# An audio-tower layer on Trainium2: score units of 28 to a sequence made 24, with a head's third and first query tile in one PSUM bank

## The reference

```python
# 1 token mixing: a causal convolution of 32 decaying taps gives 376 tokens, then two linear maps
h = _L0_tok_ref(x, Wv, bv, Wo, bo, decay_w)
# 2 attention, 16 heads of 16 features, causal, on the normalised h
q, k, v = (split(_layernorm(h) @ w + b) for w, b in ((wq, bq), (wk, bk), (wv, bv)))
scores = einsum('bhqd,bhkd->bhqk', q, k) / sqrt(16)
weights = softmax(where(tril(ones((s, s))), scores, -inf))
h = h + einsum('bhqk,bhkd->bhqd', weights, v).reshape(b, s, d) @ wo + bo
# 3 a feed-forward part: 2 shared experts and 16 routed ones, top 2 of a token
h = h + _L0_ffn_ref(_layernorm(h), ...)
```

## Time and profile before

| | |
|---|---|
| median of three runs | 1868.26 us (1855.72 to 1869.14) |
| span of the profiled execution | 1852.8 us |
| PE busy | 1700.5 us, 92% of the span |
| DVE busy | 1437.1 us, 78% |
| POOL busy | 1056.0 us, 57% |
| ACT busy | 976.7 us, 53% |

### The profile page before, as it was taken

How to read it: one execution, slowest core, us unless ns; L and a number is a source line. 1 busy time by engine, 2 the same in 40 slices (tenths; PEclk the granted TensorE clock), 3 DMA queues, 4 the chain that set the end, 5 groups by cost and what they waited for, 6 DMA issues and landing times. The chain is left out here.

```text
span 1852.8 us, 49530 instructions
## 1 busy us (share of the span) xinstructions
PE 1700.5 (92%) x14718; PEld 1360.0 (73%) x14719; DVE 1437.1 (78%) x3985; ACT 976.7 (53%) x2048; POOL 1056.0 (57%) x1446
## 2 busy tenths in 40 slices
PE   5899999999999999999999998589999986988883
PEld 4677777777777777777777775368888876877773
DVE  4589899999999899899999996378888971455554
ACT  1166666666676666666666765333444422544441
POOL 4045555555555655655555556446777770567666
PEclk8899999999999999999999999679999997999996
DMA  2555556556556555555565453223333356999996
GB/s 76 80 132 152 141 128 158 142 119 166 141 135 144 147 147 138 135 154 142 123 162 141 123 147 99 109 74 105 126 120 120 122 155 169 286 327 326 323 331 220
DMA packets 226548, 291.13 MB, mean 157 GB/s; under 512 B 57142, under 2 KB 188954, under 8 KB 226458
## 3 DMA queue, kind: packets, MB, share of 16 engines
q1 hardware_dynamic: 190042, 186.14, 40.3%
q0 software_dynamic: 18048, 49.31, 8.2%
q10 hardware_dynamic: 18368, 54.64, 7.7%
HBM read 83.25 MB, written 129.69 MB: 115 GB/s over the span
## 5 line engine op out<-in xcount | busy, mean ns | idle before, releaser
L752 ACT ACTIVATE probs<-bank 128x376 f32<-128x376 f32 (+2 forms) x896 | 440.7, 529 | 272.9 <-PE bank L621 261.0
L843 DVE TENSOR_REDUCE neg_max<-bank 120x1 f32<-120x376 f32 (+2 forms) x896 | 507.0, 587 | 53.7 <-PE bank L587 49.7
L587 PE MATMUL bank<-k_rows,q_rows 64*128 64x128 f32 (+2 forms) x1536 | 403.7, 345 | 3.1 <-ACT probs L752 2.4
L621 PE MATMUL bank<-q_rows,k_rows 64*120 64x120 f32 (+2 forms) x1536 | 369.9, 336 | 3.9 <-ACT probs L752 3.6
L982 POOL TENSOR_SCALAR_AFFINE_SELECT probs<-probs 128x512 f32<-128x512 f32 (+1 forms) x384 | 232.4, 631 | 209.5 <-ACT probs L752 209.3
L604 PE MATMUL bank<-causal,own_row 56*120 56x56 bf16 (+4 forms) x1792 | 300.9, 248 | 8.7 <-DMA k_rows<-k_flat_hi 3.5
L587 PEld LDWEIGHTS bank<-k_rows,q_rows 64*128 64x128 f32 (+1 forms) x1536 | 246.2, 186 | 6.7 <-ACT probs L752 4.6
L2205 POOL DMA_INDIRECT y_got<-y_sorted,p_route x188 | 182.4, 970 | 119.7 <-issue 117.6
L621 PEld LDWEIGHTS bank<-q_rows,k_rows 64*128 64x128 f32 (+1 forms) x1536 | 229.8, 183 | 8.7 <-ACT probs L752 5.8
L604 PEld LDWEIGHTS bank<-causal,own_row 64*128 64x128 bf16 (+2 forms) x1792 | 153.4, 115 | 110.3 <-DVE neg_max L843 39.9
L1847 POOL DMA_INDIRECT x_sorted<-r_normed,route x188 | 184.3, 981 | 83.6 <-issue 59.0
(11 more groups left out here) (235 smaller groups left out, 4148.8 us busy)
## 6 DMA issues: line engine op xcount, KB each, us to landing
x_sorted<-zeros ACTq DMA_DIRECT2D x32, 816.0 KB, 3.8
y_sorted<-zeros ACTq DMA_DIRECT2D x32, 816.0 KB, 4.3
x_rows<-x_sorted SPq DMA_DIRECT2D x51, 512.0 KB, 6.4
y_sorted<-p_y_rows SPq DMA_DIRECT2D x51, 512.0 KB, 6.4
q_rows<-q_flat_hi SPq DMA_DIRECT2D x256, 94.0 KB
k_rows<-k_flat_hi SPq DMA_DIRECT2D x248, 94.0 KB
q_rows<-q_flat_lo SPq DMA_DIRECT2D x128, 94.0 KB
out_dram<-base SPq DMA_DIRECT2D x47, 256.0 KB, 5.0
```

Of the source, the lines that this page charges most:

```text
L587: last = eng.matmul(ps[0:T[t], m * w:(m + 1) * w], q[rows, slot, t * P:t * P + T[t]], k[rows, slot, 0:w], start=False, stop=(m == len(head ...
L621: last = eng.matmul(ps[0:T[t], m * w:(m + 1) * w], k[64 * c:64 * c + 64, slot, t * P:t * P + T[t]], q[64 * c:64 * c + 64, slot, t * P:S], ...
L752: eng.activation(probs[g % 2][0:T[t], first:first + len(heads), OFF[t]:OFF[t] + w], bank_exp[n % 2][0:T[t], 0:len(heads) * w].rearrange("k ...
L843: eng.tensor_reduce(dst, src, AX.X, ALU.max, negate=True).then_inc(max_taken, 1)
```

## The change

A group has 6 units in place of 7. The first two hold two heads' middle tiles each. Each of the other four holds the third and the first query tile of one head: for the maxima 376 columns (384 with the mask's) and 128, for the exponential 376 and 120 columns, next to each other in the bank and in `probs`, so that one ACTIVATE of 496 columns does both. The reduce over such a bank gives four partial maxima, and a small reduce at the head of `turn_maxima` joins three of them. The rows of k and the last query tile are padded to 128, so that no matmul of scores has a shorter tile. Dense blocks stand at other units: conv0 and conv1 are now together at unit 7, ahead of the transposes; hid0 and hid1 are together; q0 and q1 are together at 13; k0 and k1 at 15. The order of POOL's masks is 1, 0, 2, the first two pieces of a reciprocal move, and `load_x` moves ahead in SP's queue.

```diff
-    GROUPS, UNITS = 4, 7
+    GROUPS, UNITS = 4, 6
-    OFF = [0, CUT[0], CUT[0] + CUT[1]]
+    OFF = [0, CUT[0] + CUT[2], CUT[0]]
-        k_rows = [sb(f"k_rows{p}", [P, 8, S], F32R) for p in range(2)]
+        k_rows = [sb(f"k_rows{p}", [P, 8, SPAN], F32R) for p in range(2)]
-        neg_max = sb("neg_max", [P, NT, 2, 8])
+        neg_max = sb("neg_max", [P, 2, 8, 6])
-                return (["hid0", "hid1"] * front + ["val0"] * maxima
+                return (["hid0", "hid1"] * front + ["val0"] * maxima + ["conv0", "conv1"] * mix
                         + ["nT0", "nT1", "q0", "q1", "k0", "k1"] * front
-                        + ["out0", "out1"] * finish + ["conv0", "conv1"] * mix + ["val1"] * maxima)
+                        + ["out0", "out1"] * finish + ["val1"] * maxima)
-        MAX_UNITS = [(0, (0, 1, 2, 3)), (1, (0, 1)), (1, (2, 3)), (2, (0,)), (2, (1,)), (2, (2,)), (2, (3,))]
...
+        PAIRS = 2
+        VALUES_AT = (3, 11, 16, 21)
...
                 def scores_for_max(st, g, u, m):
+                    if u < PAIRS:
+                        slot, t, at = 4 * (g // 2) + 2 * u + m, 1, 2 * P * m
+                    else:
+                        slot, t, at = 4 * (g // 2) + u - PAIRS, (2, 0)[m], NT * P * m
+                    keys = min(S, (t + 1) * P)
+                    last = eng.matmul(ps[:, at:at + keys], q[rows, slot, t * P:(t + 1) * P], k[rows, slot, 0:keys],
+                                      start=False, stop=(m == 1), skip_group_check=True)
...
                 def exps(st, g, u):
+                    if u < PAIRS:
+                        dst = probs[g % 2][:, 2 * u:2 * u + 2, OFF[1]:OFF[1] + CUT[1]]
+                        src = bank_exp[n % 2][:, 0:2 * CUT[1]].rearrange("k (m w) -> k m w", m=2)
+                    else:
+                        dst = probs[g % 2][:, u - PAIRS, 0:CUT[0] + CUT[2]]
+                        src = bank_exp[n % 2][:, 0:CUT[0] + CUT[2]]
+                    eng.activation(dst, src, ACT.Exp).then_inc(exp_done, 1)
...
                 def maxima(st, g, u):
+                    if u < PAIRS:
+                        src = max_bank(n)[:, 0:4 * P].rearrange("q (m w) -> q m w", m=2)
+                        dst = neg_max[:, half, 4 * e + 2 * u:4 * e + 2 * u + 2, 4]
+                    else:
+                        src = max_bank(n)[:, 0:4 * P].rearrange("q (c w) -> q c w", c=4)
+                        dst = neg_max[:, half, 4 * e + u - PAIRS, 0:4]
...
                 def turn_maxima(st, half, shift):
+                    eng.tensor_reduce(neg_max[:, half, :, 5], neg_max[:, half, :, 0:3], AX.X, ALU.min).then_inc(max_joined, 1)
+                    eng.wait_ge(max_joined, done)
...
                 # PE, step
-                        if n == 7 and st.maxima:
+                        if n == 5 and st.maxima:
                             values(st, 0)
+                        if n == 7 and st.mix:
+                            conv(st, 0)
+                            conv(st, 1)
                         if n == 9 and st.front:
                             normed_T(st, 0)
                             normed_T(st, 1)
-                        if n in (13, 15) and st.front:
-                            query_key(st, "q", (13, 15).index(n), w_q)
-                        if n == 17 and st.front:
+                        if n == 13 and st.front:
+                            query_key(st, "q", 0, w_q)
+                            query_key(st, "q", 1, w_q)
+                        if n == 15 and st.front:
                             query_key(st, "k", 0, w_k)
                             query_key(st, "k", 1, w_k)
-                        if n in (20, 22) and st.finish:
-                            out_rows_(st, (20, 22).index(n))
-                        if n in (24, 27) and st.mix:
-                            conv(st, (24, 27).index(n))
-                        if n == 27 and st.maxima:
+                        if n in (18, 20) and st.finish:
+                            out_rows_(st, (18, 20).index(n))
+                        if n == 23 and st.maxima:
                             values(st, 1)
...
                 # DVE
-                HALF_1_AT = {10: (0, 1), 12: (2,), 14: (3,), 16: (4,)}
-                HALF_0_AT = {21: (0,), 23: (1, 2), 25: (3,), 26: (4,)}
+                HALF_1_AT = {9: (0,), 11: (1,), 12: (2, 3), 13: (4,)}
+                HALF_0_AT = {19: (0,), 21: (1,), 22: (2, 3), 23: (4,)}
...
                 # POOL
-                            for t in reversed(range(NT)):
+                            for t in (1, 0, 2):
                                 mask(st, g, t)
```

More of the change, by code:

```diff
@@ L468, in attention_phase @@
         assert LOOP_FROM + 2 * LOOPS + 2 < B
-        MAX_UNITS = [(0, (0, 1, 2, 3)), (1, (0, 1)), (1, (2, 3)), (2, (0,)), (2, (1,)), (2, (2,)), (2, (3,))]
[L476 to L480, removed]
+        PAIRS = 2
+        VALUES_AT = (3, 11, 16, 21)
         def max_bank(n):
-            return bank_max[1 if n == LAST_UNIT else n % 3]
-        def units_since_same_bank(n):
-            return {0: 4, 1: 2, 2: 4, LAST_UNIT: 2}.get(n, 3)
+            return bank_max[n % 3]
         with nc.Block() as block:
@@ L595, in hide_later_keys @@
                     ps = max_bank(g * UNITS + u)
-                    t, heads = MAX_UNITS[u]
-                    w, d, m = KEYS_OF[t], T[t], len(heads)
                     rows = slice(64 * (g % 2), 64 * (g % 2) + 64)
+                    if u < PAIRS:
+                        blocks = ps[:, 0:4 * P].rearrange("q (m w) -> q m w", m=2)[:, :, P:2 * P]
+                    else:
+                        blocks = ps[:, 2 * P:4 * P].rearrange("q (m w) -> q m w", m=2)
                     for h in (1, 0):
[L601 to L604, removed]
+                        eng.matmul(blocks[:, :, 64 * h:P], own_row[rows, h, :], causal[rows, h, 0:2, 64 * h:P],
                                    start=(h == 1), stop=False, skip_group_check=True)
@@ L635, in scores @@
                         open_exp(st, g, u)
-                    for m in range(4):
-                        if st.maxima and m < len(MAX_UNITS[u][1]):
+                    for m in range(2):
+                        if st.maxima:
                             scores_for_max(st, g, u, m)
-                        if st.attend and m < len(EXP_UNITS[u][1]):
+                        if st.attend:
                             scores_for_exp(st, g, u, m)
@@ L800, in step @@
                                     eng.wait_ge(rows_loaded[(st.b + 1) % 2][h], st.turn(1, 208, 208))
-                        if st.front and n in (13, 15):
-                            j = (13, 15).index(n)
-                            take_hi(st, f"q{j}", q_flat[0][:, j, :], bias=bias_q[:, j:j + 1])
-                        if st.front and n == 17:
+                            for j in range(2):
+                                take_hi(st, f"q{j}", q_flat[0][:, j, :], bias=bias_q[:, j:j + 1])
+                        if st.front and n == 15:
                             for j in range(2):
                                 take_hi(st, f"k{j}", k_flat[0][:, j, :], bias=bias_k[:, j:j + 1])
-                        if st.mix and n in (25, 27):
-                            j = (25, 27).index(n)
-                            take_hi(st, f"conv{j}", mixed[0][:, j, :])
-                        if n == 25 and st.attend:
-                            keep(st, 2, 0)
                 run_steps(eng, step)
@@ L945, in step @@
                                 gather_sums(st, 1, -1, piece)
-                        if st.front and n in (13, 15):
-                            j = (13, 15).index(n)
-                            take_lo(st, f"q{j}", q_flat[1][:, j, :], q_flat[0][:, j, :], bias=bias_q[:, j:j + 1])
-                        if st.front and n == 17:
+                        if st.front and n == 14:
+                            for j in range(2):
+                                take_lo(st, f"q{j}", q_flat[1][:, j, :], q_flat[0][:, j, :], bias=bias_q[:, j:j + 1])
+                        if st.front and n == 16:
                             for j in range(2):
                                 take_lo(st, f"k{j}", k_flat[1][:, j, :], k_flat[0][:, j, :], bias=bias_k[:, j:j + 1])
+                        if st.finish and n in (18, 20):
+                            out_sum(st, (18, 20).index(n))
                         if st.attend and n in HALF_0_AT:
@@ L954, in step @@
                                 gather_sums(st, 0, 0, piece)
[L955 to L957 removed]
+                        if st.maxima and n == 23:
                             values(st, 1)
```

130 lines of the change are left out of this document (60 added, 70 removed).

## The result

The changed kernel takes 1927.24 us (median of five runs, 1924.08 to 1934.61); five runs of the kernel before beside it gave 1855.72 to 1869.77 us. The ratio is 1.035, with a 95% interval of 1.0309 to 1.0391: slower by about 3.5%, some 60 us. The forecast was +25 us and 1893 us; the sign is right, the size is not, and the time lies 5 us above the top of the range.

What follows compares the result with a forecast made beforehand. SP's chain was taken to bound the step: q1 read at 21.8 plus 13.2 gives 35.0 us against 34.06. Thirty steps at +0.9 (+28) and ends of -3 make +25, so 1893 us; range 1832 to 1922.

Steps and rivals of the forecast that it cites:

- PE's own work: PE's work in an attention step falls from 34.06 to about 32.0 us, perhaps 31.1 without small stalls.
- DVE's list: DVE's fixed order of work in a step: q1 read at 21.8 us, against 19.8 before; total 31.4 us.
- The waits: PE waits in a step: transposes 0.9 us for the convolution's read, k0 1.5 for q0's, third products 1.2 for masks.
- one sign of being wrong: At PE's waits in a step: waits for masks ahead of those of DMAs would show the forecast wrong.
- SP's chain: From q1 read to the four maxima DMAs landed, before the next step's first unit: 13.2 us, ends 12.3 and 13.8.
- its sentence on the zeros: In SP's chain: ACT's big stores of zeros move to units 10 and 19, away from the q rows.
- The ring of PE and POOL: PE waits about 1.2 us at 21 for POOL's masks; its step ends near 34.7, just under 35.0, adding nothing.
- The step: A full attention step takes 35.0 us in place of 34.06, +0.9 us, for 30 steps.
- The ends: The two steps without a front and the opening have no such chain and fewer units: about -3 us.

Runs made afterwards that it cites:

- the spread version: Changed kernel's 24 merged units, with dense blocks, reads, reciprocals and stores of zeros spread as in the kernel before: 1832.49 us, ratio 0.9819 to the kernel before.
- the one with early zeros: Changed kernel with ACT's store of zeros into y_sorted at unit 13 in place of 19, nothing else: 1917.86 us, ratio 1.0268.
- the early store: Changed kernel with second products with values at unit 15 and the store of zeros into y_sorted at 13: 1910.96 us, ratio 1.025.

## Why the prediction was right and wrong

The forecast put +25 us on the attention phase; it is +62.2 in the two traces. Of the 37 us between, some 14 lie in the 24 middle steps (+36.3, where 24 steps of the forecast's 35.0 make +22.6), and some 23 lie outside them (+25.9, where six such steps less 3 us make +2.6).

- **PE's own work: right.** I forecast 32.0 us a step; it is 31.65 in the step shown, and 32.0 to 32.2 in the spread version and in the one with early zeros (step less waits). A merged unit was taken at 0.415; two of them with what lies around them take 0.91 to 0.92 us.
- **DVE's list: right.** q1 read was put at 21.8 us after the step's start, and it ends at 586.28 - 564.92 (600.50 less 35.58) = 21.4, or at 22.0 if the step is counted from its first mask (599.82 less 35.58). The joining reduce, forecast 0.2, is 0.17. DVE's total, forecast 31.4, is 31.88.
- **The waits: right in their places.** Forecast 0.9, 1.5 and 1.2 for `mixed_lo`, `q_flat_lo` and the masks; measured 0.82, 1.07 and 1.09. But one sign of being wrong came true beside them: the waits for masks (12.2 us from 400 to 800) stand ahead of those for each of the DMAs (6.0 and 4.1).
- **SP's chain: this term was mis-sized.** I took 13.2 us with 13.8 as the upper end, and it is 14.2. The prediction failed at its sentence on the zeros: "these move to units 10 and 19, away from the q rows". They did, but onto the k rows and the maxima, at the end of the same chain. Without the store beside it the chain is 12.8 us, less than I took; the store added 1.4. Because the other ring closes the step soon after, this is worth only 0.33 us a step here, and 0.47 in the spread version.
- **The ring of PE and POOL: added up too low.** The text says that PE's work is 32.0, "perhaps 31.1", and that its step "would end near 34.7". With 32.0 the forecast's own waits give 32.0 + 0.9 + 1.5 + 1.2 = 35.6; 34.7 comes out only with the optimistic 31.1 (and the 33.7 that it gives on the way would make 34.9 with the wait for masks). With zeros out of the way the ring measured 35.24. So it was never "just under" SP's chain by a margin: with the late store the two are within 0.4 us, which is why removing either alone gives little, or makes it worse.
- **The step**, forecast 35.0, is 35.6. Over 30 steps that is +45 instead of +28.
- **The ends: wrong, and the largest error.** I gave them -3 us, on the ground that the opening and the last steps have no such chain and fewer units. They are not shorter: outside the 24 middle steps the phase is 26 us longer. Seven steps at 1.5 would be 10 of it, the four stretches at 1.2 GHz some 8, and some 7 at the opening and the end remain unexplained.
- **PE's clock: it fell in a few steps.** In the changed kernel PE is busy for 89%, at 2.4 GHz nearly throughout, and yet four steps held stretches of 3.4 to 6.8 us at 1.2 GHz. In the experiments with one hole of 2.4 us it was common. The Trainium skill (TensorE: Matmul & The Clock Gate, Part 1: The HAM clock gate) says that the clock follows how busy PE has been. The trace agrees in direction: three of the four stretches begin within two microseconds behind a wait at the first unit that is longer than in the other steps, and the fourth covers a wait of 2.39 us.

So the mechanism was the forecast one, chains in place of PE's work, and that the kernel would be slower was not luck. The size failed in the ends above all, then in the sum of the PE ring and in the late store on SP's chain. What stays open is the exact share of the clock in the 60 us: the four marked steps give 8 us, two of these stretches went when the store was moved; why the other two came is not shown. Open is also what each moved block costs by itself; only q0 and q1 were put together alone, and that in the kernel before.

## What to carry to other kernels

When a change saves work on an engine that was 99% busy, list every ring that goes once round a step and add each with the same, pessimistic number for the engine's own work; two rings of one length hide each other, and undoing one of two causes can make the time worse. Two neighbouring blocks that share two banks need not make a wait: k0 and k1 stand together in every version here. They cost over a microsecond where the next block needs the first one's bank before it has been read, as k0 did two units behind q0 and q1. So try the saving and the new placement apart: here one was worth -1.8% and the other +5%. And a large transfer that nobody waits for still needs a place where no short, awaited transfer is in flight.

## What the runs showed of the hardware

- Transfers of one size class do not land alike. The last row DMA of 94 KB could be used 3.7 us after its issue with the maxima ahead of it (639.49 to 643.20) and 3.8 us with the early store (586.27 to 590.06), where the stores of 256 KB landed in 2.1 to 2.2 us in the kernel before. Beside the late store of 816 KB the row DMA took nearly 5.5 us, and the issues of the maxima 3.41 in place of 2.79. Whether the 3.7 us come from the form of the copy or from the row DMAs queued ahead of it was not tried apart.
- The granted clock falls for single stretches while PE is still busy for nine tenths: 0.93 with one wait of 2.4 us a step, 1.00 with 32.9 us steps and 0.9 us of waits. A stretch costs 1.5 to 2 us in its step (37.75 against 36.26; 37.60 against 35.58).
- Neither the sum of the waits nor the longest one tells by itself what the clock does. The changed kernel stood 3.9 us a step in five places, none over 1.2 us, with the clock near 1.00. With the second products at 15 it stood 3.8 us (2.37 + 0.33 + 0.82 + 0.25), of them 2.4 in one place, with 0.93. But with the early store besides it stood only 2.5 us (0.82 + 0.79 + 0.63 + 0.25), and the clock fell in three steps of four; there, two waits of 0.6 to 0.9 us follow each other within 1.3 us at the first unit, in the steps without a fall too. With q0 and q1 together the wait of 1.5 us is the same in every step, and the clock fell in ten of the 24. Why was not tried by itself.
